# A window-attention layer followed by a spiking layer: levels scaled by powers of two, bias added by VectorE, and five spikes of eight made and added by GpSimd

## What is computed

```python
x = x + attention(group_norm(x))       # shifted 8 x 8 windows, 16 heads of 16 channels
x = x + spiking(group_norm(x))
```

```python
h = x_normed @ W.T + b                 # 256 -> 256
v = v + (h[t] - v) / 2.0               # charge (TAU is 2)
s = (v >= 1.0)                         # spike, 0 or 1
v = v * (1 - s)                        # reset to 0 where it spiked
out[t] = x[t] + s
```

## Time and profile before

| | us |
|---|---|
| Time, median of 3 runs | 521.34 |
| Lowest and highest of the 3 | 514.8, 522.15 |
| The profiled execution's own time | 513.7 |
| Span of its profile | 512.0 |

### The profile page before, as it was taken

The page is one execution under the profiler, slowest core; times in us unless marked ns, Lnnn a source line. Parts: engine busy times, 40 slices in busy tenths (PEclk is TensorE's granted clock), DMA queues, the critical chain, the costliest instruction groups (busy, mean ns, idle before and its releaser), DMA issues.

```text
span 512.0 us, 19282 instructions
## 1 busy us (share of the span) xinstructions
PE 427.2 (83%) x7848; PEld 395.4 (77%) x7848; DVE 408.6 (80%) x872; ACT 376.0 (73%) x895; POOL 277.2 (54%) x382
## 2 busy tenths in 40 slices
PE   0274769888899899988989898989899888699996
PEld 0274768888898888988979787879798877588885
DVE  8856557798789888977978888879767787588887
ACT  2365559888898888888969787979788876746560
POOL 6353448557566766675667557656756558420000
PEclk9987669999999999999989999999999998989999
DMA  6145133545646555555464555544544551023333
GB/s 218 70 100 148 52 74 98 133 115 155 158 118 150 126 135 130 144 141 135 101 151 126 134 139 136 148 116 95 122 107 112 112 110 40 22 103 125 143 130 138
DMA packets 136780, 61.56 MB, mean 120 GB/s; under 512 B 107506, under 2 KB 125172, under 8 KB 136692
## 3 DMA queue, kind: packets, MB, share of 16 engines
q1 hardware_dynamic: 136352, 60.33, 45.6%
q10 hardware_dynamic: 340, 0.01, 0.0%
HBM read 35.13 MB, written 25.17 MB: 118 GB/s over the span
## 4 chain that ended last, share of the span: by engine, by line
PE 31%; SPq 18%; ACT 14%; DMA 11%; DVE 11%; issue 8%; POOL 6%; ACTq 0%; DVEq 0%; POOLq 0%
SPq L312 13%; DMA k_stack<-k_spill1lo 4%; DMA k_stack<-k_spill0lo 3%; SPq L307 3%; PE score_ps L916 3%; PE proj_ps L927 3%; ACT k_flat L505 3%; PE pv_ps L1038 3%; PE proj_ps L916 3%; PE pv_ps L916 3%; PE score_ps L1014 3%; PE proj_ps L929 2%; PE proj_ps L928 2%; DMA k_spill0hi<-k_flat 2%; ACT v_hi L522 2%
## 5 line engine op out<-in xcount | busy, mean ns | idle before, releaser
L449 POOL TENSOR_TENSOR p_lo<-probs,p_hi 128x512 f16<-128x512 f32 x128 | 146.5, 1166 | 128.6 <-PE pv_ps L1038 69.9
L1004 PE MATMUL score_ps<-q_stack,k_stack 96*128 96x64 f16 x1024 | 86.1, 194 | 41.7 <-ACT max_rows L595 16.7
L604 ACT ACTIVATE probs<-score_ps 128x512 f32<-128x512 f32 x128 | 76.9, 601 | 45.2 <-PE score_ps L1014 44.4
L1004 PEld LDWEIGHTS score_ps<-q_stack,k_stack 96*128 96x128 f16 x1024 | 71.9, 98 | 48.7 <-ACT max_rows L595 35.1
L778 DVE TENSOR_REDUCE neg_max<-max_ps 128x16 f16<-128x1024 f32 x64 | 78.4, 1224 | 30.9 <-PE max_ps L984 29.9
L927 PE MATMUL proj_ps<-xn_hi,w_hi 128*128 128x256 f32 x256 | 78.8, 308 | 11.1 <-DVE w_lo L731 7.2
L1000 PE MATMUL score_ps<-both_parts,bias_k 128*128 128x64 f16 x1024 | 78.2, 194 | 0.0
L605 ACT ACTIVATE p_hi<-score_ps 128x512 f16<-128x512 f32 x128 | 77.3, 604 | 0.0
L772 DVE TENSOR_TENSOR v_lo<-proj_ps,v_hi 64x256 f16<-64x256 f32 x128 | 54.2, 423 | 25.7 <-ACT v_hi L522 24.0
L928 PE MATMUL proj_ps<-xn_lo,w_hi 128*128 128x256 f32 x256 | 73.9, 289 | 0.0
L929 PE MATMUL proj_ps<-xn_hi,w_lo 128*128 128x256 f32 x256 | 73.8, 288 | 0.0
(11 more groups left out here) (130 smaller groups left out, 1196.7 us busy)
## 6 DMA issues: line engine op xcount, KB each, us to landing
xc<-in_x_dram SPq DMA_DIRECT2D x32, 256.0 KB, 3.6
q_spill<-q_flat SPq DMA_DIRECT2D x32, 256.0 KB, 2.6
q_stack<-q_spill SPq DMA_DIRECT2D x32, 256.0 KB, 3.5
out_dram<-xc SPq DMA_DIRECT2D x32, 256.0 KB, 2.2
q_stack<-q_spill SPq DMA_DIRECT2D x32, 128.0 KB, 3.6
k_spill0hi<-k_flat SPq DMA_DIRECT2D x16, 128.0 KB, 2.6
k_spill0lo<-k_flat SPq DMA_DIRECT2D x16, 128.0 KB, 3.6
k_stack<-k_spill0hi SPq DMA_DIRECT2D x32, 64.0 KB, 3.2
```

What stands on the lines that cost most here:

```text
L449: pool.tensor_tensor(p_lo[p][:, quads, :, :].rearrange("p g w i -> p (g w i)"), probs[:, quads, :, :].rearrange("p g w i -> p (g w i)"), p ...
L604: act.activation(probs[:, quads, :, :].rearrange("p g w i -> p (g w i)"), score_ps[:, h, :], ACT.Exp)
L1004: pe.matmul(dst, k_stack[slot][0:96, 2 * mid + q, at, :], q_stack[slot][0:96, 2 * mid + q, at, :], start=False, stop=False)
```

## The change

The membrane and the levels are no longer halved with each step. They are kept multiplied by 2^t: with TAU = 2 the charge becomes `level = membrane + bank + bias * 2^t / 2`, with no factor on the membrane, and the threshold of step t is 2^t. For that, `norm_roots` multiplies `rstd` of the spiking layer's samples by `powers` (2^t), and `lif_bias` holds the bias column for each t.

TensorE no longer adds the bias. VectorE does so in the charge, in two instructions of 128x256 instead of one of 128x512, since each half has its own bias column; ScalarE adds it for t = 0, also in two instructions instead of one.

Of the 32 spikes 19 go to GpSimd, those with t = 1, 2, 4, 5 and 7 except the very last. GpSimd makes the spikes in a tile of their own (`spikes`, a TENSOR_SCALAR), waits for itself, and adds them to `xc` (a TENSOR_TENSOR). VectorE still adds 13. There are four level tiles instead of two (the two new ones lie in `xn`), and a bank is free when its charge is done instead of its spike.

```diff
@@ norm_roots
+            if not isinstance(norm, int) or norm >= SAMPLES:
+                eng.tensor_tensor(rstd[:, cols], rstd[:, cols], powers[:, cols], ALU.mult).then_inc(scaled, 1)
+                eng.wait_ge(scaled, norm - (SAMPLES - 1))
@@ new functions
+        def added_by_pool(y, t):
+            return t % 3 != 0 and not (y == WROWS - 1 and t == SAMPLES - 1)
+        def await_spikes(eng, y, t):
+            by_pool = added_by_pool(y, t)
+            eng.wait_ge(spikes_added if by_pool else spike_done, units_up_to(y, t, by_pool))
@@ gpsimd, after the last norm_roots
+            def lif_units(y):
+                for t in range(SAMPLES):
+                    if added_by_pool(y, t):
+                        number = units_up_to(y, t, True)
+                        wait(pool, spikes_added, number - 1)
+                        pool.wait_ge(charge_done, y * (SAMPLES - 1) + t)
+                        pool.tensor_scalar(spikes, charged[t % 4][:, :], 2.0 ** t, None, ALU.is_ge).then_inc(spikes_made, 1)
+                        pool.wait_ge(spikes_made, number)
+                        pool.tensor_tensor(one(xc, y + t * WROWS), one(xc, y + t * WROWS), spikes, ALU.add).then_inc(spikes_added, 1)
@@ scalar
-            act.wait_ge(setup_dve, 1)
-            for r in (0, 32):
-                act.dma_start(b_raw[r:r + 1, 0:C], lif_b.rearrange("(o c) -> o c", o=1)).then_inc(b_loaded, 16)
+            act.dma_start(lif_bias_raw[:, :], lif_b.rearrange("(h p) -> p h", p=128), allow_slow_non_contiguous=True).then_inc(b_loaded, 16)
-            act.activation(b_rows[:, :], b_raw, ACT.Copy).then_inc(setup_act, 1)
-                        act.activation(first_charge, banks[0], ACT.Copy).then_inc(first_done, 1)
+                        for h in range(HALVES):
+                            tok = slice(h * ROWTOK, (h + 1) * ROWTOK)
+                            last = act.activation(first_charge[:, tok], banks[0][:, tok], ACT.Identity, bias=lif_bias[:, h, 0:1])
@@ vector, setup
-            dve.memset(b_raw, 0.0).then_inc(setup_dve, 1)
-            dve.memset(ones_r[:, :].bitcast(f32), 1.0)
+            for t in range(SAMPLES):
+                dve.memset(powers[:, t * HALVES:(t + 1) * HALVES], 2.0 ** t)
-            for r in (0, 32):
-                last = dve.tensor_scalar(b_raw[r:r + 1, 0:C], b_raw[r:r + 1, 0:C], 1.0 / TAU, None, ALU.mult)
+            for t in range(SAMPLES):
+                last = dve.tensor_scalar(lif_bias[:, :, t], lif_bias_raw[:, :], 2.0 ** t / TAU, None, ALU.mult)
-            dve.tensor_tensor(b_rows[32:33, :], b_raw[32:33, :], b_rows[32:33, :].bitcast(f32), ALU.subtract).then_inc(rows_done, 1)
@@ vector, lif_units
-                        wait(dve, spike_done, y * SAMPLES + (t - 1))
+                        if t > 4:
+                            await_spikes(dve, y, t - 4)
+                        elif y > 0:
+                            await_spikes(dve, y - 1, t + 4 if t + 4 < SAMPLES else t)
-                        dve.scalar_tensor_tensor(level, membrane[:, :], 1.0 - 1.0 / TAU, banks[t], ALU.mult, ALU.add)\
-                           .then_inc(charge_done, 1)
+                        for h in range(HALVES):
+                            tok = slice(h * ROWTOK, (h + 1) * ROWTOK)
+                            last = dve.scalar_tensor_tensor(level[:, tok], membrane[:, tok], lif_bias[:, h, t:t + 1], banks[t][:, tok],
+                                                            ALU.add, ALU.add)
+                        last.then_inc(charge_done, 1)
-                        dve.scalar_tensor_tensor(membrane[:, :], level, 1.0, level,
+                        dve.scalar_tensor_tensor(membrane[:, :], level, 2.0 ** t, level,
-                    dve.scalar_tensor_tensor(one(xc, y + t * WROWS), level, 1.0, one(xc, y + t * WROWS),
+                    if not added_by_pool(y, t):
+                        dve.scalar_tensor_tensor(one(xc, y + t * WROWS), level, 2.0 ** t, one(xc, y + t * WROWS),
@@ tensor
-                    pe.matmul(dst, b_rows[:, h * 128:(h + 1) * 128], ones_r[:, :], start=True, stop=False)
-                    wait(pe, spike_done, m - 7)
+                    if y > 0:
+                        if t == 0:
+                            pe.wait_ge(first_done, y)
+                        else:
+                            pe.wait_ge(charge_done, (y - 1) * (SAMPLES - 1) + t)
```

More of the change, by code:

```diff
@@ L59, in swin_attention_then_lif_kernel @@
         w_lif = sb("w_lif", [128, HALVES, C], f32)
-        b_rows = sb("b_rows", [128, C], f32r)
+        lif_bias = sb("lif_bias", [128, HALVES, SAMPLES], f32)
+        lif_bias_raw = sb("lif_bias_raw", [128, HALVES], f32)
+        powers = sb("powers", [128, SAMPLES * HALVES], f32)
         b_cols = sb("b_cols", [128, 3 * HALVES], f32)
-        ones_r = sb("ones_r", [128, ROWTOK], f32r)
         ident = sb("ident", [128, 128], f32)
@@ L110, in swin_attention_then_lif_kernel @@
         unit = [sb(f"unit{i}", [128, HALVES * ROWTOK], f32) for i in range(4)]
-        charged = [sb(f"charged{i}", [128, HALVES * ROWTOK], f32) for i in range(2)]
+        charged = [sb(f"charged{i}", [128, HALVES * ROWTOK], f32) for i in range(2)] + [t[:, :] for t in xn]
+        spikes = sb("spikes", [128, HALVES * ROWTOK], f32)[:, :]
         first_charge = probs[:, :, :, :].rearrange("p g w i -> p (g w i)")[:, 0:HALVES * ROWTOK]
@@ L176, in swin_attention_then_lif_kernel @@
         spike_done = sem("spike_done")
+        spikes_made = sem("spikes_made")
+        spikes_added = sem("spikes_added")
+        scaled = sem("scaled")
         stored = sem("stored")
@@ L241, in is_last_y, with units_up_to @@
             return isinstance(y, int) and y == WROWS - 1
+        def added_by_pool(y, t):
+            return t % 3 != 0 and not (y == WROWS - 1 and t == SAMPLES - 1)
+        def units_up_to(y, t, by_pool):
+            return sum(added_by_pool(m // SAMPLES, m % SAMPLES) == by_pool for m in range(y * SAMPLES + t + 1))
+        def await_spikes(eng, y, t):
+            by_pool = added_by_pool(y, t)
+            eng.wait_ge(spikes_added if by_pool else spike_done, units_up_to(y, t, by_pool))
         def over_y(eng, body):
@@ L354, in store_units @@
                 for t in range(SAMPLES):
-                    sp.wait_ge(spike_done, y * SAMPLES + (t + 1))
+                    await_spikes(sp, y, t)
                     sp.dma_start(out[t, :, bass.ds(y, 1), :].rearrange("p y n -> p (y n)"), one(xc, y + t * WROWS))\
@@ L466, in _ @@
             norm_roots(pool, root_pool, SAMPLES * ROOT_STEPS, SAMPLES + 1, EARLY, HALVES)
+            def lif_units(y):
[7 more added lines that the diff above has]
+                        pool.tensor_tensor(one(xc, y + t * WROWS), one(xc, y + t * WROWS), spikes, ALU.add).then_inc(spikes_added, 1)
+            over_y(pool, lif_units)
         @block.scalar
@@ L619, in lif_units @@
                         act.wait_ge(h_ps_done, y * SAMPLES + 1)
-                        act.activation(first_charge, banks[0], ACT.Copy).then_inc(first_done, 1)
+                        if not is_first(y, 1):
+                            await_spikes(act, y - 1, 0)
+                        for h in range(HALVES):
+                            tok = slice(h * ROWTOK, (h + 1) * ROWTOK)
+                            last = act.activation(first_charge[:, tok], banks[0][:, tok], ACT.Identity, bias=lif_bias[:, h, 0:1])
+                        last.then_inc(first_done, 1)
                     if is_first(y, 1) and t == 1:
@@ L633, in _ @@
         def _(dve):
-            dve.memset(b_raw, 0.0).then_inc(setup_dve, 1)
-            dve.memset(ones_r[:, :].bitcast(f32), 1.0)
-            dve.memset(three_halves[:, :], 1.5)
+            for t in range(SAMPLES):
+                dve.memset(powers[:, t * HALVES:(t + 1) * HALVES], 2.0 ** t)
+            dve.memset(three_halves[:, :], 1.5).then_inc(setup_dve, 1)
             for slot in range(2):
@@ L858, in lif_units @@
                     m = y * SAMPLES + t
-                    level = first_charge if t == 0 else charged[t % 2][:, :]
+                    level = first_charge if t == 0 else charged[t % 4][:, :]
                     if t == 0:
@@ L913, in project_unit @@
                     dst = bank[:, h * ROWTOK:(h + 1) * ROWTOK]
-                    pe.matmul(dst, b_rows[:, h * 128:(h + 1) * 128], ones_r[:, :], start=True, stop=False)
                     for c in range(HALVES):
                         last = pe.matmul(dst, w_lif[:, c, h * 128:(h + 1) * 128], tokens[:, c * ROWTOK:(c + 1) * ROWTOK],
-                                         start=False, stop=(c == HALVES - 1))
+                                         start=(c == 0), stop=(c == HALVES - 1))
                 return last
```

12 lines of the change are left out of this document (4 added, 8 removed).

## The result

| | before | changed |
|---|---|---|
| Time, median of the runs | 518.07 us (4 runs, 513.94 to 522.15) | 523.59 us (4 runs, 521.01 to 526.38) |
| Ratio to before, 95% interval | | 1.0134 (1.0082 to 1.0186), slower by 7 us |
| Span of the profiled execution | 512.0 | 522.0 |
| First reset of the spiking layer to the end of the span | 69.8 | 77.4 |

The account below looks back on a forecast made before the run. TensorE was taken to bound the spiking layer before, VectorE waiting behind GpSimd after. 513.7 + 4.2 = 517.9 us against the profiled execution; the median lies 7.6 above that execution, so 525.5; range 511 to 534.

Parts of the forecast that it names:

- What bounds it before: Spiking layer before the change: TensorE sets the pace at 1.96 us a unit, 15.7 a row, with VectorE close behind.
- TensorE, after: TensorE's half unit loses the 0.21 us bias load: a unit falls from 1.96 to 1.54, a row to 12.3.
- The charge: VectorE's charge as two 128x256 instructions of about 0.48 us: 0.88 a pair against 0.69 now, bounds 0.84 and 0.95.
- GpSimd's pair: GpSimd's two instructions per moved spike: compare taken as 0.60 us, add as 1.27.
- So whoever comes second waits for the other's whole instruction: VectorE's two-SBUF-input instructions and GpSimd's block each other; behind one, a reset adds 0.55 us, GpSimd's add 1.13.
- The sum: Spiking layer unit by unit, VectorE waiting behind GpSimd: steps of 2.36 us, a row 16.3 against 15.7, layer +4.2.
- The last row and the end: Last row of the spiking layer: 17.1 us from its first reset, ending at 513.5 against 509.27.
- The setup: Memsets, scalings and a dropped subtraction before the first norm: net -0.3 to +0.7 us, taken as 0; bias DMA 0, at most +2.
- Free overlap: Rival: VectorE and GpSimd share no port at this size, VectorE row 12.8 us, total -9.5 to 511.8; chance 0.20.
- The dear compare: Rival: GpSimd's compare is slower than assumed, +10.4 us at 0.93, ending near 0.97; typically +12, 533; chance 0.18.
- TensorE's clock: Rival: TensorE, a quarter idle, falls to its lower clock; a row of 24.6 us, +30; chance 0.05.
- the first rival: Rival that VectorE and GpSimd overlap freely in the spiking layer: -9.5 us, 511.8; chance 0.20.

## Why the prediction was right, and where not

- **What bounds it before.** Right. TensorE at 1.96, VectorE close.
- **TensorE, after.** Mis-sized: 0.42 less a unit, measured 0.23 (1.73). The bias load overlaps passes of the unit; the chain had the true price, 0.12 a half. It did no harm, since TensorE was off the path either way.
- **The charge.** Right: pairs of 0.87, never stretched.
- **GpSimd's pair.** This step failed. "I take 0.60" for the TENSOR_SCALAR; it is 1.49, above the 1.27 that I gave as the bound from above. Here a two-input instruction of the same engine was no upper bound for a one-input one, and the affine select was the wrong neighbour.
- **"So whoever comes second waits for the other's whole instruction."** Right for the add, in both directions: a spike that began in an add ended 0.55 after it, and the add of 466.26 ended 1.14 after the spike of 466.25, as forecast (1.13). Right for the copy. Wrong for the compare, which held VectorE up for 0.44 of its 1.49 at most. I had generalised from TENSOR_TENSORs, the only GpSimd instructions in the rows that met anything.
- **The sum.** The steps of 2.36 are right where their price is (2.37 with the copy). In the change itself the bound moved: not VectorE behind GpSimd (16.3) but GpSimd's queue (16.8). That it came out near is luck: the compare costs GpSimd 0.9 more than assumed, and lets the resets of VectorE pass, which nobody had foreseen. The 525.5 is nearer to the 523.59 than its parts are: the base of 521.34 was 3.3 above the 518.07 that before has with a fourth run, and the layer's loss 3.4 too small.
- **The last row and the end.** The row was longer than forecast (18.6 for 17.1) because the end waits for GpSimd's backlog, and the stores behind it add 1.4. Together that is about 3 of the 3.4 us by which the layer's sum was short.
- **The setup.** "0, at most +2": the bias column's DMA made VectorE wait 0.65, and the first maximum came 0.26 later than before.
- **The rivals.** Free overlap: excluded. The dear compare came true, beyond its stated point; that the order would then turn over and the loss shrink again was right, to 7.6 us in the layer rather than 4. TensorE's clock: granted at 1.00 in rows 1 and 2 of the changed kernel too; it fell in row 3 (0.50 from 506 us on), after TensorE's last matmul.
- **The signs.** Charges stayed at 0.48, as forecast. Three signs did not come: no reset took 1.4, compares took 1.81 and not 1.05, first resets lay 16.8 apart and not 16.3. One misled: resets at 0.69 were to give the first rival. They stayed at 0.69 to 0.74 and that rival was wrong as well, because a compare that costs much and holds VectorE up little was not among the cases. The sign that the whole sum would be wrong, a compare over 0.97, came.

The Trainium skill (SBUF: State Buffer, "SBUF: two separate sides") has the second comer blocked for the whole instruction. By the adds this case agrees (a wait of 1.07 of the add's 1.27); by the compares it does not (a reset begun 0.02 after a compare was through 0.34 before it), and the measurement decides. The same skill calls one-input work on GpSimd "roughly line-rate" (GPSIMD Engine Reference, "Engine selection"). The copy at 0.61 fits that; the TENSOR_SCALAR at 1.49 does not.

## What to carry to other kernels

A spike costs VectorE 0.61 us; moved to GpSimd it costs GpSimd 2.9, frees only 0.39 where the next charge then follows its reset, and, if the add meets a two-input instruction of VectorE, costs VectorE 1.07 as well. Before elementwise work is moved to GpSimd, price the exact instruction form there, count the queue that it makes with its collisions (five pairs were 14.6 us bare and 16.8 with them, in a row of 15.7), and place its two-input instructions beside VectorE's PSUM work: the same two moved spikes cost 1.7 us a row more or less by their place alone. And when an engine's share is relieved, take the price from the chain, not from the start of the next load.

## What the runs showed of the hardware that was not expected

- A GpSimd TENSOR_SCALAR of 128x512 takes 1.49 us, in f32 and in f16, compare or multiply; a copy 0.61, a two-input add 1.27.
- Such a TENSOR_SCALAR kept a VectorE instruction with two SBUF inputs waiting 0.44 us at most in these runs; a copy and an add keep it waiting to their end. It is itself stretched by one that is under way (to 2.0 us).
- A one-input fp32 VectorE instruction (the doubling, 0.41 us alone) also gets longer: it takes up to 0.83 beside compares and 1.48 beside adds.
- A bias matmul costs TensorE 0.12 us a half in fp32r and 0.11 in f16, though its weight load is half as long (0.10 for 0.19).

**Open.** The attention layer took 442 us in the profile of before and 442 to 454 in the others. The edits need not be the reason: the kernel before alone ran from 510.5 us at a mean granted clock of 0.98 to 528.9 at 0.94. In the profiles, too, the length goes with TensorE's granted clock up to the first reset: 442 to 445 us at 0.97, 442 to 450 at 0.96, 451 to 454 at 0.95 or 0.94. Which is cause and which effect no run shows. An estimate of what is lost ahead of row 1 is the ratio's share of 517 us, less the difference from row 1 on: 0.5 to 5.5 us against before for the experiments that have a ratio, most for the one without GpSimd, and nothing for the changed kernel. Most of these are more than the 0.3 that the setup explains, and near what the intervals allow. No run settles whether that is real.
